# Eight-stage transformer block on one core: the layer normalisations of four stages written as two steps, statistics and application, with other work between them

## What is computed

```
def _layernorm(x, axis=-1, eps=1e-05):
    m = jnp.mean(x, axis=axis, keepdims=True)
    v = jnp.var(x, axis=axis, keepdims=True)
    return (x - m) / jnp.sqrt(v + eps)

x = _layernorm(x + _L0_attn_ref(x, ...))
x = _layernorm(x + _L0_ffn_ref(x, ...))
x = _layernorm(x + _L1_attn_ref(x, ...))
x = _layernorm(x + _L1_ffn_ref(x, Wg, W1, W2, W3))      # experts
x = _layernorm(x + _L2_attn_ref(x, ...))
x = _layernorm(x + _L2_ffn_ref(x, w1_w, ..., w3_s))     # ternary
x = _layernorm(x + _L3_attn_ref(x, Wq, ..., rel_v_table)) # clipped
x = _layernorm(x + _L3_ffn_ref(x, w_gate, ..., w2_s))   # routed
```

## Time and profile before

| | us |
|---|---|
| median of three runs | 2226.43 |
| lowest and highest of the three | 2225.49, 2232.22 |
| the profiled execution, its own time | 2229.38 |
| its span, first to last instruction | 2227.7 |
| mean granted TensorE clock in it | 0.973 of full speed |

### The profile page before, as it was taken

One profiled execution on the slowest core, in us unless ns is written; L12 is line 12 of the kernel. 1 busy time (PEld: TensorE's weight loads), 2 busy tenths in 40 slices (PEclk: granted clock), 3 DMA queues, 4 the chain that ended last, 5 costly groups with the idle time before them and its releaser, 6 DMA issues.

```text
span 2227.7 us, 44943 instructions
## 1 busy us (share of the span) xinstructions
PE 1999.3 (90%) x17759; PEld 1183.2 (53%) x17759; DVE 1448.8 (65%) x2865; ACT 1105.7 (50%) x1926; POOL 821.1 (37%) x1161
## 2 busy tenths in 40 slices
PE   6888789989978999998998899999799899999888
PEld 3343466666644454555665444445465665665556
DVE  6775678888678777764555875121677676767574
ACT  2564356555513454564222466222576675757442
POOL 4654434333137847441001421000545344453133
PEclk9999999999989999999999999999999999999999
DMA  3430111111234434211002320000565564655252
GB/s 126 148 105 2 30 30 30 27 32 30 84 92 124 139 91 134 76 34 66 40 1 63 97 81 12 33 0 1 168 210 173 172 205 138 207 167 176 58 116 57
DMA packets 183993, 199.15 MB, mean 89 GB/s; under 512 B 55922, under 2 KB 152486, under 8 KB 179302
## 3 DMA queue, kind: packets, MB, share of 16 engines
q1 hardware_dynamic: 183782, 196.27, 30.0%
HBM read 93.53 MB, written 92.08 MB: 83 GB/s over the span
## 4 chain that ended last, share of the span: by engine, by line
PE 34%; DVE 6%; ACT 5%; issue 5%; DMA 2%; POOL 2%; SPq 1%; DVEq 0%; ACTq 0%; POOLq 0%
PE PS L2167 5%; PE PS L365 4%; PE PS L2418 3%; PE PS L2434 3%; PE PS L2406 3%; ACT AR L2578 2%; PE PS L2015 2%; PE PS L2002 2%; PE PS L2005 2%; PE PS L2773 1%; PE PS L640 1%; PE PS L2761 1%; PE PS L2763 1%; PE PS L619 1%; PE PS L2176 1%
## 5 line engine op out<-in xcount | busy, mean ns | idle before, releaser
L1326 ACT ACTIVATE AR<-PS 128x1024 f32<-128x1024 f32 x160 | 162.5, 1024 | 122.0 <-PE PS L1077 121.1
L762 ACT ACTIVATE AR<-PS 128x1024 f32<-128x1024 f32 x160 | 162.5, 1023 | 93.8 <-PE PS L619 45.7
L1181 DVE TENSOR_REDUCE AR<-PS 128x2 f32<-128x768 f32 (+1 forms) x192 | 159.9, 864 | 46.3 <-PE PS L1056 23.0
L2634 POOL TENSOR_TENSOR RA<-AR,RA 128x288 f32<-128x288 f32 x128 | 88.0, 698 | 273.0 <-DVE RA L2510 140.2
L2578 ACT ACTIVATE AR<-PS,AR 128x512 f32<-128x512 f32 x256 | 173.9, 687 | 27.5 <-DVE AR L2499 26.3
L2499 DVE TENSOR_REDUCE AR<-PS 128x2 f32<-128x1024 f32 x128 | 156.8, 1225 | 13.3 <-DVE PS L2496 0.5
L2406 PE MATMUL PS<-AR 64*128 64x200 f32 (+2 forms) x1280 | 145.5, 351 | 2.2 <-ACT AR L2578 2.2
L1884 POOL TENSOR_TENSOR AR<-AR 128x1024 f32<-128x1024 f32 x32 | 75.5, 2358 | 173.6 <-DVE AR L1737 173.6
L2418 PEld LDWEIGHTS PS<-CC,AR 64*128 64x128 f32 x2048 | 77.4, 140 | 98.3 <-issue 78.2
L2418 PE MATMUL PS<-CC,AR 64*128 64x64 f32 x2048 | 91.9, 229 | 39.0 <-ACT AR L2562 12.0
L2406 PEld LDWEIGHTS PS<-AR 64*128 64x128 f32 x1280 | 110.0, 191 | 5.7 <-ACT AR L2578 2.2
(11 more groups left out here) (359 smaller groups left out, 5005.1 us busy)
## 6 DMA issues: line engine op xcount, KB each, us to landing
ZD<-RC SPq DMA_DIRECT2D x32, 1152.0 KB
AR<-ZD SPq DMA_DIRECT2D x32, 640.0 KB
ZP<-AR SPq DMA_DIRECT2D x128, 160.0 KB, 2.7
SP<-AR SPq DMA_DIRECT2D x40, 384.0 KB, 2.6
AR<-SP SPq DMA_DIRECT2D x128, 96.0 KB
RA<-SP SPq DMA_DIRECT2D x32, 384.0 KB
SP<-AR SPq DMA_DIRECT2D x40, 256.0 KB, 2.9
RC<-RC SPq DMA_DIRECT2D x64, 130.0 KB
```

The lines of the kernel that those rows point to most:

```text
L762: e.activation(self.PT[m % 6], C.PS[:, 2 * s:2 * s + 2, :], ACT.Exp).then_inc(S["s_turned"].sem, 1)
L1181: i = e.tensor_reduce(nm[:, :, 4 * up + q:4 * up + q + 1], src[:, :, a:a + wd], AX, ALU.max, negate=True)
L1326: e.activation(self.PT[m % 6], C.PS[:, 2 * s:2 * s + 2, :], ACT.Exp).then_inc(S["s_turned"].sem, 1)
L2634: e.tensor_tensor(self.XM[:, 2 * q:2 * q + 2, :], self.PP[n % 5][:, :, 128 * q:128 * q + 144], W["edge"].unsqueeze(1).broadcast_to((128, 2 ...
```

## The change

`normalise_vector` is cut in two. `normalise_stats` does the statistics and the addition, `normalise_apply` waits for the factor and applies it. In Experts, Ternary, Clipped and Routed the step `fin` becomes two steps, `ln` (statistics, and the factor on POOL or ACT) and `fin` (application), and other steps of the plan are laid between them. The operations and their shapes are the same. In Clipped `turnx` moves with `fin` by a turn, except in the last batch. In Routed the last batch's `gate6`, `send` and `rep` move from behind `hidden` 21 to behind `hidden` 22, and so from ahead of the first `outward` to behind it. Three lists at the joins of two stages grow by one or two steps, so that their steps are interleaved a little differently.

```diff
-def normalise_vector(e, w, vs, ss, key, y, st, dst):
+def normalise_stats(e, w, vs, key, y, st):
...
-    at = vs.per - 4
-    w.wait_ge(vs, *key, part=at + 1)
+    w.wait_ge(vs, *key, part=1)
...
+def normalise_apply(e, w, vs, ss, key, y, st, dst):
+
     w.wait_ge(ss, *key)
...
# Experts
                 plan.append(("outward", m))
                 if m % 8 == 7:
-                    plan.append(("fin", m // 8))
+                    plan.append(("ln", m // 8))
+            if n % 16 == 2 and n > 16 or n == 16 * NB:
+                plan.append(("fin", (n - 16) // 16))
...
-            w.wait_ge(S["v_outward"], 8 * b + 7)
-            normalise_vector(e, w, S["v_fin"], S["g_fin"], key, C.YB[:, b % 2, :], C.ST[:, b % 2, :], C.XK[:, b, :])
+            normalise_apply(e, w, S["v_fin"], S["g_ln"], key, C.YB[:, b % 2, :], C.ST[:, b % 2, :], C.XK[:, b, :])
...
# Ternary
-            self.plan += [("hidden", 4 * b + c) for b in (pair, pair + 1) for c in range(4)]
+            for n in range(4 * pair, 4 * pair + 8):
+                self.plan.append(("hidden", n))
+                if n == 9:
+                    self.plan.append(("fin", 1))
...
-            for b in (pair, pair + 1):
-                self.plan += [("outward", b), ("fin", b)]
+            self.plan += [("outward", pair), ("ln", pair), ("outward", pair + 1), ("fin", pair), ("ln", pair + 1)]
+            if pair:
+                self.plan.append(("fin", pair + 1))
...
# Clipped
                 if m == 2:
+                    plan.append(("ln", b))
+                if m == (2 if b == NB - 1 else 4):
                     plan.append(("fin", b))
-                if m == 4:
+                if m == (4 if b == NB - 1 else 6):
                     plan.append(("turnx", b))
...
# Routed
-            when.setdefault(5 * b + 6, []).extend([("gate6", b), ("send", b), ("rep", b)])
+            when.setdefault(5 * b + (7 if b == NB - 1 else 6), []).extend([("gate6", b), ("send", b), ("rep", b)])
...
                 b = (21, 29, 35).index(n)
-                plan += [("outward", b), ("fin", b)]
+                plan.append(("outward", b))
+            if n in (22, 30):
+                plan.append(("ln", (22, 30).index(n)))
+            if n in (24, 32):
+                plan.append(("fin", (24, 32).index(n)))
         b = NB - 1
-        return plan + [("scale", b, c) for c in range(8)] + [("outward", b), ("fin", b)]
+        return plan + [("ln", b - 1), ("fin", b - 1)] + [("scale", b, c) for c in range(8)] + [("outward", b), ("ln", b), ("fin", b)]
```

More of the change, by code:

```diff
@@ L339, in normalise_vector @@
     i.then_inc(vs.sem, 1)
-    w.wait_ge(vs, *key, part=at + 2)
+    w.wait_ge(vs, *key, part=2)
     e.tensor_scalar_add(st[:, 32:36], st[:, 25:32:2], 1e-5).then_inc(vs.sem, 1)
+def normalise_apply(e, w, vs, ss, key, y, st, dst):
     w.wait_ge(ss, *key)
@@ L346, in normalise_vector @@
     i.then_inc(vs.sem, 1)
+def normalise_vector(e, w, vs, ss, key, y, st, dst):
+    normalise_stats(e, w, vs, key, y, st)
+    normalise_apply(e, w, vs, ss, key, y, st, dst)
 def normalise_scalar(e, w, vs, ss, key, st):
-    w.wait_ge(vs, *key, part=vs.per - 1)
+    w.wait_ge(vs, *key, part=3)
     e.activation(st[:, 40:44], st[:, 32:36], ACT.Ln).then_inc(ss.sem, 1)
@@ L1956, in __init__ @@
             "t": {"gate1": 1, "hidden": 2, "outward": 1, "turnx": 1},
-            "v": {"gate1": 2, "gate2": 3, "gate3": 6, "hidden": 1, "outward": 4, "fin": 4},
+            "v": {"gate1": 2, "gate2": 3, "gate3": 6, "hidden": 1, "outward": 4, "ln": 3, "fin": 1},
             "s": {"gate2": 1, "hidden": 1, "turnx": 1},
-            "g": {"fin": 1},
+            "g": {"ln": 1},
         }
@@ L2107, in on_gpsimd @@
         C, S, key = self.C, self.S, step[1:]
[L2108 removed]
+        normalise_gpsimd(e, C, w, S["v_ln"], S["g_ln"], key, C.ST[:, key[0] % 2, :])
 class Ternary:
@@ L2136, in __init__ @@
             "t": {"hidden": 2, "inner": 1, "outward": 1, "turnx": 1},
-            "v": {"hidden": 1, "outward": 2, "fin": 4},
+            "v": {"hidden": 1, "outward": 2, "ln": 3, "fin": 1},
             "s": {"hidden": 1, "inner": 1, "turnx": 1},
-            "g": {"fin": 1},
+            "g": {"ln": 1},
         }
@@ L2234, in on_gpsimd @@
         C, S, key = self.C, self.S, step[1:]
-        normalise_gpsimd(e, C, w, S["v_fin"], S["g_fin"], key, C.ST[:, key[0] % 2, :])
+        normalise_gpsimd(e, C, w, S["v_ln"], S["g_ln"], key, C.ST[:, key[0] % 2, :])
 class Clipped:
-    tables = {"exp": EXPS, "fin": EXPS}
+    tables = {"exp": EXPS, "ln": EXPS}
     head, tail, past, sent = 0, 0, None, ("lay", "skew", "band", "gather", "send", "rep")
@@ L2276, in __init__ @@
                   "wo": 1, "turnx": 1, "turn": 1, "table": 1},
-            "v": {"init": 2, "vals": 1, "scores": 2, "backv": 1, "xsum": 1, "sums": 2, "close": 1, "wo": 1, "fin": 4},
-            "s": {"turn": 1, "table": 1, "q": 1, "k": 1, "rel": 1, "exp": 1, "backs": 1, "wt": 1, "fin": 2, "turnx": 1},
+            "v": {"init": 2, "vals": 1, "scores": 2, "backv": 1, "xsum": 1, "sums": 2, "close": 1, "wo": 1, "ln": 3, "fin": 1},
+            "s": {"turn": 1, "table": 1, "q": 1, "k": 1, "rel": 1, "exp": 1, "backs": 1, "wt": 1, "ln": 2, "turnx": 1},
             "g": {"init": 1, "qr": 2, "k": 1, "vals": 1, "band": 1, "wo": 1},
@@ L2530, in on_vector @@
             e.tensor_tensor(y, y, o[:, 0:128], ALU.add).then_inc(S["v_wo"].sem, 1)
+        elif kind == "ln":
+            b, = key
+            w.wait_ge(S["v_wo"], b, 3)
+            normalise_stats(e, w, S["v_ln"], key, C.YB[:, b % 2, :], C.ST[:, b % 2, :])
         elif kind == "fin":
             b, = key
-            w.wait_ge(S["v_wo"], b, 3)
-            normalise_vector(e, w, S["v_fin"], S["s_fin"], key, C.YB[:, b % 2, :], C.ST[:, b % 2, :], C.XK[:, b, :])
+            normalise_apply(e, w, S["v_fin"], S["s_ln"], key, C.YB[:, b % 2, :], C.ST[:, b % 2, :], C.XK[:, b, :])
     def on_scalar(self, e, w, step):
@@ L2593, in on_scalar @@
                          ACT.Copy).then_inc(S["s_wt"].sem, 1)
-        elif kind == "fin":
+        elif kind == "ln":
             b, = key
-            normalise_scalar(e, w, S["v_fin"], S["s_fin"], key, C.ST[:, b % 2, :])
+            normalise_scalar(e, w, S["v_ln"], S["s_ln"], key, C.ST[:, b % 2, :])
         elif kind == "turnx":
@@ L2680 @@
 class Routed:
-    tables = {"gate1": SIGM, "hidden": SILU, "fin": EXPS}
+    tables = {"gate1": SIGM, "hidden": SILU, "ln": EXPS}
     head, tail, past, sent = 0, 0, None, ("send", "rep")
```

18 lines of the change are left out of this document (14 added, 4 removed), and 4 rows, old and new, of the table cv.

## The result

The changed kernel takes **2209.01 us** (median of 4 runs, 2205.86 to 2210.47), the kernel before 2227.44 (2225.49 to 2232.22): ratio **0.9902**, 95% interval 0.9884 to 0.9919. The profiled execution took 2208.0 us, with a span of 2206.3.

A forecast was written before the change was run, and what follows sets the result against it. PE was taken to bound the kernel, so gains come only where PE waits; terms for Experts, Ternary, Clipped, Routed and joins summed to 21.2 us, from 2229.4 to 2208.2, median 2205, range 2200 to 2215.

The forecast's parts named there:

- Experts, stalls and clock: Experts, batches 0 to 2: shorter PE stalls save 6.1 us, two avoided half-speed stretches 3.4.
- the clock doesn't come back: Rival: stalls go but half-speed stretches fall elsewhere, so 14.6 us gained, 2212; chance 0.20.
- Ternary's first pair: Ternary, batches 0 and 1: PE's stall falls from 1.64 to about 0.6, gain 1.0 us.
- Join of Ternary and Clipped: Where Ternary meets Clipped: POOL's `vals` tiles start earlier, gain 0.8 us, bounds -2 to +1.5.
- The sign named for it: Join of Ternary and Clipped: the second `skew` awaited some 1 us less long.
- Clipped, stalls, clock and the join with Routed: Clipped: stalls save 4.6 us, the clock 3.2; the join with Routed costs 0.4.
- that rival: Rival: Clipped is held by DMA round trips, its 7.8 us become `skew` and `rep` waits, 2213; chance 0.12.
- Routed: Routed: 2.5 us gained, 1.8 of it PE's wait at `gate6` 3; bounds 0 to 3.
- the normalisation of batch 0: Routed: it costs PE 0.39 us and as much again at the next matmul; 0.8 saved, less 0.4 for a late product.
- The slower rival: Rival: applications beside POOL's tiles take up to 6.3 us, making the kernel 12 us slower, 2239; chance 0.04.
- one sign of a wrong prediction: The prediction is wrong if applications beside POOL take over 3 us.
- Table loads: Routed, around ACT's factor: 1.28 us per table load, covered by three pairs of banks.

The follow-up runs named there:

- the repetition: The changed kernel run again, unedited: 2214.18 us, ratio 0.9927 to the kernel before.
- the filled kernel: The kernel before with nine useless bf16 matmuls on PE in each of the three batch-end stalls of Experts: 2226.63 us, 0.9976.
- experts_only: The kernel before with normalisation split in Experts alone: 2222.61 us, 0.996.
- clipped_only: The kernel before with normalisation split in Clipped alone, `turnx` a turn later: 2222.43 us, 0.9964.
- ternary_only: The kernel before with normalisation split in Ternary alone: 2227.6 us, 0.9986.
- the edited kernels: The changed kernel with Routed's `outward` 0 behind `hidden` 19 (2211.99 us), or behind 26 with POOL's batch 0 `scale` tiles after batch 3's gate (2207.37 us).
- early_outward: The changed kernel with Routed's `outward` 0 behind `hidden` 19 instead of 21 and `gate6` 3 behind 20 instead of 22: 2211.99 us, 0.9901.

## Why the prediction was right

The time for an execution like the profiled one was forecast at 2208.2, and the profiled execution took 2208.0; for the median 2205 stands against 2209.01. By the ratio the gain is 1 - 0.9902 of 2227.44, 21.8 us, and in the repetition 0.0073, 16.3. The forecast's gain was 21.2.

The mechanism came true where most of the gain lies, in the stalls and the clock of Experts and Clipped. That 2208.2 met 2208.0 so closely is luck: 1.3 of the measured 21.4 lie outside the touched stretches, and the terms below miss in both directions. And the forecast for the median took over that it was 3.0 below the profiled execution before; after the change it is 1.0 above it, which is the 4 us between 2205 and 2209.01.

Term by term, with means over the traces where single ones scatter:

- **Experts, stalls and clock**: forecast 6.1 + 3.4 = 9.5; measured 10.17 in every pair of traces, 6.9 and 3.3 by the filled kernel. The step held. With 0.07 left of each stall it would be 6.4 + 3.4; the other 0.4 of the stage I haven't placed.
- **The rival "the clock doesn't come back"** fell: none in 126 us after the change, and the filled kernel gets 3.3 with the stalls' delay left in. What spoke for it was the one stall of three without a drop; in the four other traces with this Experts it is another one. The places say nothing; the count repeats.
- **Ternary's first pair**: 1.0 forecast, 1.24 measured, the same in all four rows of the table with this part.
- **Join of Ternary and Clipped**: 0.8 forecast. What repeats is that POOL is through the eight `vals` tiles and starts the second `qr` 23.98 behind T2 instead of 24.50, 0.52 sooner, in every kernel with this part. Against more stands the application, which takes 3.03 beside POOL's tiles, with PE's wait of 1.67 behind it; what each of these costs isn't separated. The sign named for it failed, since the second `skew` is awaited as long as before, 5.15 for 5.12, and not some 1 us less. Over T2 to C0, kernels of the table with the split give 190.9 to 193.3 and those without 190.5 to 194.2, so that the 0.52 reaches the end isn't shown.
- **Clipped, stalls, clock and the join with Routed**: 4.6 + 3.2 - 0.4 = 7.4. C0 to C3 is 377.98 on average in the six traces of the table with an unsplit Clipped, and 370.58 in the four with a split one: 7.4. The stalls are 0.69, not 0.8, and the gain didn't turn into DMA waits, so that rival fell as well. But the equal sum is partly luck. Three stalls, each shorter by 1.6, make 4.9, and the drops behind them, 14 in the six traces, cost 4.0 us on average, where the forecast counted two drops. That makes 8.9, so about 1.5 was lost in between, most of it behind batch 2, where the forecast had 0.4 for the join with Routed.
- **Routed**: 2.5 forecast, 0.9 in the first pair of traces. The mechanism was right (`gate6` 3 without a wait); the term missed the waits of the gate steps behind POOL's `scale` tiles, of which the trace of before happened to show one of two. In the five traces with the old Routed C3 to R3 is 103.26 on average, in the three with the new 101.11: 2.15. Some 0.8 of that is clock, a term that I had put at nothing: three of the five have a drop behind the waits (0.76 over 7 us in `experts_only` and `clipped_only`, 0.66 over 10 in `ternary_only`), of the three new ones only the repetition has one. The reason given for 0.7 of the forecast, the normalisation of batch 0, isn't shown: from the first statistics of Routed (R0) to R3 it is 48.1 to 48.5 us with the split, whose R0 stands one `hidden` of 1.72 later in the work, so it compares as 49.8 to 50.2 with 49.2 to 50.2 without.
- **The slower rival** had its price right and its place wrong. I set 4.6 us for an application as the point from which it decides; 1.89 came in Clipped, 3.03 at the join, 2.65 to 3.08 in Routed, and 4.13 and 5.14 in the edited kernels. So one sign of a wrong prediction, applications over 3 us, did show, and the time was faster all the same: the sign was set too low, since most of them lie where PE doesn't wait. The Trainium skill ("SBUF — State Buffer", section "Who interferes with whom") says that a DVE instruction in its fast two-port mode and a POOL instruction lock each other out of one shared pair of ports, and that one with two inputs from SBUF contends with a POOL instruction that reads SBUF. The rows agree: two-input steps of 16 to 32 columns take 0.97 to 1.30 beside a tile of 1.28 and 0.17 to 0.20 without, a reciprocal stays at 0.18, and the products, with one input in PSUM, at 0.69. Where the rival erred is that it let these prices reach PE: in the changed kernel they did so in the gates, which the change doesn't touch, and of the applications only in the one at the join (1.67, a place where PE had waited 2.18 before); in `early_outward` in one more (1.29).
- **Table loads**: 1.28 as counted. The load at 2154.80 is followed by an activation at 2156.09 and PE waits for ACT nowhere from 2107 on. The dearer switch that the Trainium skill gives ("ScalarE: Activation LUTs", section "What ACT_TABLE_LOAD costs") didn't appear.

## What to carry to other kernels

A chain through a second engine in the middle of an in-order queue costs its wait and its own time wherever the bounding engine wants the next thing behind it. Cut it at the wait and put the second half where that queue has idle time; the gain can then be summed from the stalls and the clock behind them (in Experts 9.5 us forecast and 10.17 measured). Before comparing two traces, look at which stretches repeat to hundredths in kernels with the same code and which vary by microseconds: one trace decides on the first alone. If POOL streams over SBUF, keep chains of tiny instructions off its time (the gate: 0.97 to 1.30 us for steps of 0.17 to 0.20) and let covered ones meet it.

## What the runs showed of the hardware

- Stalls of TensorE of only 2.15 to 2.28 us, in an otherwise busy stage, were followed by stretches at 1.2 GHz in two of three cases in all five traces, and not always in the same ones; stalls of 2.31 and 2.32 in Clipped in two or three of three. Filled with useless matmuls the stalls of Experts weren't, for 3.3 us per three stalls. The wait of 2.65 had the same behind it (0.76 over 7 us), while the waits of 2.12 and 2.00 in the changed kernel's gates had not (1.00 from 2134 to 2148).
- Four `tensor_scalar` of 128 columns took 1.11 us alone and 1.89, 2.66, 3.03, 3.08, 4.13 and 5.14 beside POOL's tiles: 5.14 is one POOL tile of 1.2 to 1.3 us for each.
- A gate step of 4 to 32 columns took 0.97 to 1.30 us instead of 0.17 to 0.20 beside the same tiles, and PE waited 4.1 us in that batch; with POOL's tiles put behind the gate the steps took 0.17 and 0.18, and both waits were gone.
